# Laying out the biases of a linear-attention layer: one f32r product over 64 rows in place of an fp32 product over 128

## The reference

```
h = layernorm(x)
q = h @ Wq + bq ; k = h @ Wk + bk ; v = h @ Wv + bv
q, k = softmax over the 8 features of each head
for (qf, kf) in ((feat(q), feat(k)), (feat(1 - q), feat(1 - k))):
    kv = kf^T v ; z = 1 / max(qf . sum(kf), eps) ; attn += qf kv z
x = x + attn @ Wo + bo
```

## Time and profile before

| what | value |
|---|---|
| median of three runs | 507.46 us (506.75 to 507.61) |
| profiled execution, its own time | 509.59 us |
| span of its trace | 507.9 us |
| granted TensorE clock, mean over the span | 0.959 of full |
| instructions in the trace | 8227 |
| stage "at1", first token transpose to output projection | 163.89 to 213.50 us in the span |

### The profile page before, as it was taken

One profiled execution on the slowest core, in us unless ns is written; L12 is line 12 of the kernel. 1 busy time (PEld: TensorE's weight loads), 2 busy tenths in 40 slices (PEclk: granted clock), 3 DMA queues, 4 the chain that ended last, 5 costly groups with the idle time before them and its releaser, 6 DMA issues.

```text
span 507.9 us, 8227 instructions
## 1 busy us (share of the span) xinstructions
PE 443.4 (87%) x2660; PEld 340.5 (67%) x2660; DVE 345.4 (68%) x943; ACT 308.4 (61%) x603; POOL 144.5 (28%) x210
## 2 busy tenths in 40 slices
PE   1898999978983898579899797999999999999994
PEld 1576777747731686447777665687878787878783
DVE  3567777696379575557777767858676776768663
ACT  1577677541255433035666466877787878787881
POOL 7282201222065100034644431222222222222222
PEclk9999999998797899859999999999999999999998
DMA  8214441000400000001111002020202112020201
GB/s 298 66 39 143 128 140 31 1 1 1 166 1 0 1 1 1 0 9 33 35 30 25 23 1 83 0 86 0 84 1 85 32 52 82 1 83 1 85 1 41
DMA packets 14053, 24.03 MB, mean 47 GB/s; under 512 B 4000, under 2 KB 10784, under 8 KB 12608
## 3 DMA queue, kind: packets, MB, share of 16 engines
q1 hardware_dynamic: 13584, 22.71, 13.9%
q10 hardware_dynamic: 432, 0.85, 0.4%
HBM read 19.29 MB, written 0.59 MB: 39 GB/s over the span
## 4 chain that ended last, share of the span: by engine, by line
PE 34%; issue 7%; DVE 6%; POOL 2%; ACT 2%; DMA 1%; SPq 0%; POOLq 0%; DVEq 0%
PE ps L1662 5%; PE ps L1664 4%; PE ps L1663 4%; PE ps L1697 4%; PE ps L1698 4%; PE ps L1696 4%; POOL xnT L502 2%; DVE masked L911 2%; PE ps L1372 2%; PE ps L1329 2%; PE ps L1339 1%; PE ps L1639 1%; DVE odif L946 1%; ACT bigr L763 1%; PE ps L1384 1%
## 5 line engine op out<-in xcount | busy, mean ns | idle before, releaser
L1163 DVE TENSOR_TENSOR bigr<-ps,bigr 128x512 fp32r<-128x512 f32 x128 | 86.1, 689 | 51.6 <-ACT ps L764 51.6
L763 ACT ACTIVATE bigr<-ps,b 128x512 fp32r<-128x512 f32 x128 | 89.9, 702 | 32.3 <-PE ps L1664 32.3
L626 ACT ACTIVATE big<-ps 128x512 f32<-128x512 f32 (+1 forms) x128 | 69.0, 550 | 47.8 <-PE ps L1339 46.2
L764 ACT ACTIVATE ps<-ps,b 128x512 f32<-128x512 f32 x128 | 86.7, 678 | 0.0
L502 POOL TENSOR_TENSOR xnT<-xnT,big 128x512 f32<-128x512 f32 x32 | 41.4, 1293 | 148.7 <-DVE big L1171 148.7
L1329 PE MATMUL ps<-bigr,qk 128*128 128x256 f32 (+1 forms) x256 | 62.5, 331 | 7.4 <-DVE nmax L918 2.7
L1662 PE MATMUL ps<-k1hi,w1hi 128*128 128x512 f32 x128 | 52.8, 412 | 2.7 <-DVE bigr L1163 2.2
L1329 PEld LDWEIGHTS ps<-bigr,qk 128*128 128x128 f32 x256 | 40.3, 195 | 21.6 <-issue 12.8
L918 DVE TENSOR_REDUCE nmax<-ps 128x2 f32<-128x512 f32 x64 | 42.7, 688 | 17.3 <-PE ps L1329 16.8
L1696 PE MATMUL ps<-bigr,w2hi 128*128 128x512 f32 x128 | 51.1, 399 | 0.0
L1664 PE MATMUL ps<-k1lo,w1hi 128*128 128x512 f32 x128 | 50.6, 396 | 0.0
(11 more groups left out here) (194 smaller groups left out, 800.9 us busy)
## 6 DMA issues: line engine op xcount, KB each, us to landing
big<-gates SPq DMA_DIRECT2D x8, 1024.0 KB, 4.6
bigr<-qk SPq DMA_DIRECT2D x112, 32.0 KB, 1.8
wi<-in_wi SPq DMA_DIRECT2D x4, 512.0 KB, 4.3
wo<-in_wo SPq DMA_DIRECT2D x4, 512.0 KB, 4.5
big<-in_sel SPq DMA_DIRECT2D x1, 1024.0 KB, 8.7
wo<-in_w SPq DMA_DIRECT2D x1, 1024.0 KB, 4.8
wi<-in_w SPq DMA_DIRECT2D x1, 1024.0 KB, 7.0
x<-in_x SPq DMA_DIRECT2D x1, 512.0 KB, 4.8
```

Source lines behind the costliest of these rows:

```text
L626: act.activation(prob[:, h % 8, c], ps[:, 2 + h % 2, c], ACT.Exp, scale=DH ** -0.5).then_inc(s(L + "_exp"), 1)
L763: act.activation(ghi[:, u % 2, c, :], ps[:, c, :], ACT.Gelu_apprx_tanh, bias=b1[:, u % E1, c:c + 1])
L764: act.activation(ps[:, c, :], ps[:, c, :], ACT.Gelu_apprx_tanh, bias=b1[:, u % E1, c:c + 1]).then_inc(s("ff1_gel"), 1)
L1163: v.tensor_tensor(glo[:, u % 2, c, :], ps[:, c, :], ghi[:, u % 2, c, :].bitcast(f32), ALU.subtract).then_inc(s("ff1_glo"), 1)
```

## The change

The bias product becomes f32r, a format of 4 bytes per element that TensorE takes in one record for each product. Two bands of rows are used: the bias rounded to f32r in partitions 0 to 31 and what the rounding leaves out in partitions 32 to 63. The stationary operand `bias_rows` has ones in rows 0 and 32 and 64 rows in all, so the product is again the bias, the sum of both parts. POOL makes the new operands where it made `first_row`. The tiles' own products stay fp32.

```diff
+        biases = sb("biases", [2 * QUAD, 3, D], f32r)
+        bias_rows = sb("bias_rows", [2 * QUAD, P], f32r)
...
-            pool.memset(first_row[0:1, :], 1.0).then_inc(s("zeroed"), 1)
+            for row in (0, QUAD):
+                pool.memset(first_row[row:row + 1, :], 1.0).then_inc(s("zeroed"), 1)
+            pool.wait_ge(s("zeroed"), 3)
+            pool.wait_ge(s("ld_at1"), 8 * 16)
+            pool.tensor_copy(bias_rows[:, :], first_row[0:2 * QUAD, :]).then_inc(s("zeroed"), 1)
+            pool.wait_ge(s("zeroed"), 4)
+            pool.tensor_copy(biases[:, :, :], bqkv1[0:2 * QUAD, :, :]).then_inc(s("zeroed"), 1)
+            pool.wait_ge(s("zeroed"), 5)
+            rest = slice(QUAD, 2 * QUAD)
+            pool.tensor_tensor(biases[rest, :, :], bqkv1[rest, :, :], biases[rest, :, :].bitcast(f32), ALU.subtract
+                               ).then_inc(s("zeroed"), 1)
+            pool.wait_ge(s("zeroed"), 6)
...
-            pe.wait_ge(s("zeroed"), 2)
+            pe.wait_ge(s("zeroed"), 6)
...
-                pe.matmul(ps[:, 0, :].rearrange("p (t c) -> p t c", t=TPB), first_row[:, :],
-                          bqkv1[:, 0:2, :].rearrange("p a d -> p (a d)").unsqueeze(1).broadcast_to([P, TPB, 2 * D]),
-                          start=True, stop=False)
+                pe.matmul(ps[:, 0, :].rearrange("p (t c) -> p t c", t=TPB), bias_rows[:, :],
+                          biases[:, 0:2, :].rearrange("p a d -> p (a d)").unsqueeze(1)
+                          .broadcast_to([2 * QUAD, TPB, 2 * D]), start=True, stop=False)
...
-                pe.matmul(ps[:, 1, 0:TPB * D].rearrange("p (t c) -> p t c", t=TPB), first_row[:, :],
-                          bqkv1[:, 2, :].unsqueeze(1).broadcast_to([P, TPB, D]), start=True, stop=False)
+                pe.matmul(ps[:, 1, 0:TPB * D].rearrange("p (t c) -> p t c", t=TPB), bias_rows[:, :],
+                          biases[:, 2, :].unsqueeze(1).broadcast_to([2 * QUAD, TPB, D]), start=True, stop=False)
```

## The result

The changed kernel is slower: 510.38 us median (509.55 to 512.31, seven runs) against 507.61 us (506.49 to 508.89, seven runs), a ratio of 1.0049 with a 95% interval of 1.0029 to 1.0069. The forecast was 2.3 us faster; by the two ratios the kernel is 2.5 and 1.9 us slower, half a per cent or less, but clear of the noise.

The account below looks back on a forecast made before the run. Stage "at1" was taken as bound by batch 0's half-clock hand-overs, then by TensorE without idle time. Batch terms 1.1 + 0 + 0.94 + 0.28 gave 2.3 us off 507.46, so 505.2 us, range 503.4 to 506.8.

Parts of the forecast that it names:

- What bounds the kernel: Stage "at1": batch 0's hand-overs among TensorE, ACT and DVE at clock 0.50, then TensorE busy 20.00 of 20.2 us.
- Batch 0: Start of stage "at1" at half clock: values done at 169.32 instead of 170.40, 1.1 us won, bounds 1.0 and 1.7.
- batch 2: Bias products in TensorE's stretch without idle time: all 0.94 us counts, with 0.6 us margin to DVE's normalisation.
- batch 3: Ahead of batch 2's plain side: only 0.28 us won, the other 0.66 becoming a wait for DVE.
- the forecast wait: TensorE, at batch 2's plain side, would newly wait about 0.7 us for DVE.
- batch 1: Projections before batch 0's plain side: 0 won, 0.94 us becoming a wait for DVE's normalisation.
- the price of the new product: f32r bias products on TensorE: 0.23 and 0.12 us at full clock, at most 0.43 and 0.22; 0.94 us gained per batch.
- the prediction's own conditions: Wrong if the clock's rise moves, L1621's duration changes, or TensorE waits for DVE in batch 2.
- Rival 3: Stage start: a shorter TensorE run makes the clock rise later, so the kernel is slower, 508.5 us; chance 0.07.
- POOL and DVE: POOL's added work, at most 3.2 us, fits in 7.56 us idle; price 0, at most 0.3 for DVE sharing.
- Rival 1: Output projection L1621 starts early enough to escape the slow clock: 1.6 us more won, 503.6 us; chance 0.17.
- rival 2: Gain mostly swallowed: batch 0 or 2 term lost, dearer f32r product (0.43), DVE loss; about 506.8 us; chance 0.18.

Follow-up runs that it names:

- e1: Changed kernel with its f32r bias operands on all 128 rows (rows 64 to 127 zeros): 505.04 us, ratio 0.9964 to the kernel before.
- e11: The changed kernel with f32r bias operands on 128 rows, repeated in a second job: 506.76 us, ratio 0.9948 to the kernel before.
- e12: 128-row f32r kernel with TensorE made to wait for its own last product on either side of each bias product: 513.71 us, ratio 1.0102 to the kernel before.
- e6: Changed kernel with 11 unused fp32 products in TensorE's idle time ahead of the stage: 506.8 us, ratio 0.9964 to the kernel before.
- e2: Kernel before with its fp32 bias products cut to 64 rows, nothing else: 514.6 us, ratio 1.0136 to the kernel before.
- e4: Changed kernel with both bias products of a batch beside each other, two row-height changes instead of four: 507.08 us, ratio 0.9989 to the kernel before.
- e9: Changed kernel with f32r bias products on 128 rows in batches 0 and 1, 64 rows in 2 and 3: 508.26 us, ratio 0.9985 to the kernel before.
- e10: Changed kernel with f32r bias products on 64 rows in batches 0 and 1, 128 rows in 2 and 3: 510.05 us, ratio 1.0019 to the kernel before.
- e5: Kernel before with 11 unused fp32 products in TensorE's idle time ahead of the stage: 507.63 us, ratio 0.9983 to the kernel before.
- e7: 128-row f32r kernel with 11 unused fp32 products in TensorE's idle time ahead of the stage: 504.64 us, ratio 0.9931 to the kernel before.

## Why the prediction was wrong

**What bounds the kernel** was read rightly: the path of batch 0 at half clock, then TensorE without idle time. e1, which keeps the row height, follows the sum term by term against the trace that the sum was made from. Batch 0's plain side came 1.09 us sooner (forecast 1.1), batch 2 gained 0.94 (0.94), batch 3 gained 0.33 (0.28) with the forecast wait of L1569 for DVE's L1079 (0.45 us), batch 1 nothing. Some of that agreement is luck: against the two other traces of the kernel before (plain side at 10.6 and 10.5) batch 0 gains 0.8, and of the 2.36 us that e1 has won by batch 2's plain side 1.95 are left at the output projection. The ratios of e1 and e11 come to 1.8 and 2.6 us; 2.3 was the sum.

**The step that failed** is the price of the new product: "I take 0.23, and half of it, 0.12, for 256 columns", with the upper bound of "half of the fp32 price". I priced the product by an f32r product of 128 rows among others of 128 rows and took the 64 rows for a detail of the operand. What they cost doesn't lie in the product but in the weight loads beside it, 0.20 us of the batch for each of four changes. At full clock a batch gained 0.15 us in place of 0.94, below the 0.64 that I had called the least. With it fell "Batch 0: 1.1 us" (its products gained 0.09) and "Batch 1: 0": at half clock batch 1's products took 4.22 us and not 3.04, ended after DVE's normalisation, and put batch 0's plain side 1.09 us later, where 1.1 sooner was forecast.

The trace of before had a row that I didn't weigh. In attention, 128 x 32 stationary operands stand beside 128 x 128 ones (there the columns change, not the rows), and the load behind the change waits:

```profile
90.86 0.59 PEld L1372 LDWEIGHTS ps<-big,vaug 128*32 128x32 f32 x16
91.86 0.42 PEld L1384 LDWEIGHTS ps<-ident,big 128*128 128x128 f32 x4 [0.41 <-issue]
```

That would have been the nearest row for a change of shape. Its 0.41 us is idle time of the loads and not yet a price, but it would have put the gain of 0.94 in doubt; at the 0.20 us measured since, four changes take 0.79 of it.

**The clock.** "I take 1.1, since in the new kernel TensorE would still be streaming at 169.2" failed with it: its products still followed one another, but the loads around the 64-row ones were not hidden, and the clock was at 0.50 until 12.1 us. That the clock's rise would not move was one of the prediction's own conditions. Rival 3 said that the clock would rise later and that this is slower; it was given 0.07 and is what happened, at 12 to 15 us after the first transposes in place of 5. Its ground was another (a shorter run of work), and that ground does not carry the delay: the run with 128 rows is shorter still, and the clock rose at 5.2 us in e1 and at 8.1 in e11. What put it off to 12 and more were the gaps, as e12 shows without any 64 rows.

The Trainium skill ("TensorE: Matmul & The Clock Gate", Part 2, the step on weight loads) says that a weight load is pulled ahead of matmuls in flight when their row groups don't conflict or when it goes to a background buffer, and that its length doesn't depend on the number of rows. The traces agree on the length (0.18 us for 64 rows, 0.19 for 128). They show the pulling ahead between loads of the same row height; a load of another row height is not pulled ahead here, and starts with its own matmul.

**POOL and DVE** went as forecast: DVE's additions beside POOL's new work (L967, at 92.01 and 94.03) took 0.29 us each, as before. Rival 1 did not occur (the output projection still took 3.79 us; in e6, where the clock stayed up, it took 2.05, near the 1.9 of the rival's price). Of rival 2 the waits did not occur, but its dearer product did, and beyond the bound of 0.43 that it was given.

**What stays open.** The loss, 1.9 and 2.5 us by the two ratios, is not the sum of fixed terms. In three pairs of traces the stage is 1.1 to 4.3 us longer, with the clock's moment and its second fall, and the later stages differ too. The division between those was not measured, nor why the clock rises at 5 us in one trace with 128 rows and at 8 in another. e2, e4, e6, e9, e10 and e12 have one trace each.

## What to carry to other kernels

Keep the row height of the stationary operand the same along a stream of matrix products: in e1 the zero rows cost nothing, and a change of height costs a weight load that isn't hidden, 0.20 us of the batch at full clock here. Price a new instruction with its neighbours, not alone: look in the trace for a row in which the same two shapes meet. Where a stage begins at the slow clock, ask of a change whether it puts gaps into the run that would raise it; here the same gaps cost some 3.6 us in the two batches at the slow clock and 1.9 in the two at full clock, if the noise is set aside. The mended version, f32r on 128 rows, is faster than the kernel before, by 0.4 to 0.5%, and so than the changed one.

## What the runs showed of the hardware that was not expected

- A weight load of 64 rows between 128-row products, and the load of 128 rows behind it, start only with their own matmul (178.20 and 178.63 in the changed kernel), at 0.20 us for each change of height in e1, e2 and e4; of two 64-row loads in a row the second runs beside the first one's matmul, 0.11 us after the first load (e4).
- With such gaps around the bias products of the first two batches TensorE stayed at 1.2 GHz until 11.5 to 18.7 us after the first transposes, in seven traces (in e12 the gaps are waits around 128-row products); without them the clock rose at 4.8 to 8.1 us, in eight traces. In e6, already at 2.4 GHz, the gaps did not bring it down.
- Eleven idle-time products, about 7 us of work, kept the clock up into the stage in one trace (e6) and not in two others (e5, e7), with the same 0.90 us of idle time behind them.
